# One step in 72 of an edge loop gets its table rows through SyncE, row by row

## The reference

```python
q = (X @ Wq)[src]
k = (X @ Wk)[dst]
e = jnp.tanh(q + k)                      # 64 wide
scores = e @ Wphi
exp_scores = jnp.exp(scores - jnp.max(scores))
denom = segment_sum(exp_scores, src)
alpha = exp_scores / (denom[src] + 1e-09)
msg = alpha[:, None] * ((X @ Wy_w + Wy_b)[dst] + e @ We)
out = segment_sum(msg, src)
return layernorm(x + out)
```

## Time and profile before

| what | us |
|---|---|
| median of 3 runs (5638.15, 5648.86, 12187.95) | 5648.86 |
| profiled execution | 5649.77 |
| its span in the trace | 5648.0 |

### The profile page before, as it was taken

One profiled execution on the slowest core, in us unless ns is written; L12 is line 12 of the kernel. 1 busy time (PEld: TensorE's weight loads), 2 busy tenths in 40 slices (PEclk: granted clock), 3 DMA queues, 4 the chain that ended last, 5 costly groups with the idle time before them and its releaser, 6 DMA issues. The chain is left out here.

```text
span 5648.0 us, 99340 instructions
## 1 busy us (share of the span) xinstructions
PE 4178.2 (74%) x26293; PEld 3164.3 (56%) x26293; DVE 3638.0 (64%) x8199; ACT 2776.5 (49%) x10974; POOL 3497.5 (62%) x3560
## 2 busy tenths in 40 slices
PE   7899999995676666666666666666766666676677
PEld 6745555553555555555555555555555555555556
DVE  6588888886555555555555555555555555655556
ACT  3488888884343344444444444444444434434346
POOL 1022333233777777777777777777777777777771
PEclk9956666665877777777777777778777777777778
DMA  2200000002333333333333333333333333333334
GB/s 85 70 4 4 4 4 5 4 4 59 105 105 105 105 104 105 105 105 105 105 105 105 105 105 105 105 105 105 105 106 105 105 104 105 105 105 105 105 98 108
DMA packets 279601, 478.59 MB, mean 85 GB/s; under 512 B 91964, under 2 KB 198878, under 8 KB 278814
## 3 DMA queue, kind: packets, MB, share of 16 engines
q0 software_dynamic: 166144, 326.27, 21.7%
q1 hardware_dynamic: 95132, 140.96, 7.8%
q10 hardware_dynamic: 17794, 4.91, 0.4%
HBM read 456.42 MB, written 20.60 MB: 84 GB/s over the span
## 5 line engine op out<-in xcount | busy, mean ns | idle before, releaser
L1015 POOL DMA_INDIRECT gathered<-table,dst_rows x3296 | 3156.7, 958 | 1035.0 <-issue 967.3
L1050 PE MATMUL bank<-gathered,weighted_onehots 128*128 128x193 f32 x6592 | 1793.8, 432 | 364.1 <-DVE block_sums L1122 350.4
L1039 PE MATMUL bank<-q_parts,src_onehots_T 128*128 x9888 | 1136.3, 216 | 983.9 <-DVE src_onehots_T L1084 728.8
L1050 PEld LDWEIGHTS bank<-gathered,weighted_onehots 128*128 128x128 f32 x6592 | 1497.5, 255 | 420.9 <-ACT weighted_onehots L1070 347.1
L1039 PEld LDWEIGHTS bank<-q_parts,src_onehots_T 128*128 128x128 bf16 x9888 | 870.0, 107 | 1410.0 <-issue 1208.6
L1122 DVE TENSOR_TENSOR block_sums<-block_sums,bank 128x193 f32 x3296 | 1166.1, 354 | 527.3 <-issue 193.6
L1059 ACT ACTIVATE gathered<-gathered 128x256 f32<-128x256 f32 x824 | 346.0, 420 | 2190.3 <-DVE gathered L1098 2190.3
L1070 ACT ACTIVATE weighted_onehots<-src_onehots,edge_weight 128x128 f32<-128x128 bf16 x3296 | 1073.4, 396 | 26.8
L1098 DVE TENSOR_TENSOR gathered<-bank,gathered 128x256 f32<-128x256 f32 x824 | 349.5, 424 | 1125.8 <-DMA gathered<-table,dst_rows 1107.6
L797 ACT ACTIVATE places_past_far<-bank,stat 128x98 bf16<-128x98 f32 x2727 | 887.3, 401 | 130.0 <-DVE place_col L780 93.0
L839 POOL DMA_INDIRECT sorted_list<-sorted_groups,unit_destinations x248 | 319.7, 1289 | 813.3 <-DVE sorted_groups L767 749.5
(11 more groups left out here) (180 smaller groups left out, 2248.7 us busy)
## 6 DMA issues: line engine op xcount, KB each, us to landing
src_in_block_rows<-src_in_block_list SPq DMA_DIRECT2D x206, 512.0 KB, 3.8
gathered<-table,dst_rows POOLq DMA_INDIRECT x3296
table<-in_x SPq DMA_DIRECT2D x4, 1562.5 KB
x_in<-in_x SPq DMA_DIRECT2D x24, 256.0 KB, 2.9
x_again<-in_x SPq DMA_DIRECT2D x48, 128.0 KB, 2.3
out<-out_rows SPq DMA_DIRECT2D x48, 128.0 KB, 1.9
sorted_list<-sorted_groups,unit_destinations POOLq DMA_INDIRECT x248, 2.5
table<-k_and_q ACTq DMA_DIRECT2D x24, 128.0 KB, 2.0
```

The costliest lines, as they stand in the source:

```text
L1015: e.indirect_dma_start(slot[:, r, j, 0:ROW], None, table, bass.IndirectOffsetOnAxis(ap=gidx[:, t:t + 1].bitcast(u32), axis=0)).then_inc(ga ...
L1039: made = e.matmul(QK[q % 2][:, j * A:(j + 1) * A], ohT[:, c % 2, o:o + PARTS], q3[:, bass.ds(b + s_ * A, A)], start=s_ == 0, stop=s_ == 2)
L1050: made = e.matmul(SM[q % 2 * 2 + j // 2][:, o:o + SUMS], ohw[:, q % 3, j, :], slot[:, r, j, A:SLOT], start=True, stop=True)
```

## The change

The last step of each period of 72 steps (PERIOD = 18 chunks) is no longer fetched by POOL. For these NSP = 11 steps (71, 143, ..., 791) SyncE issues 512 DMAs of one row each, 5,632 in all, into a sixth slot that only they use. Each takes its row number from a register. 16 registers are loaded at a time from `rows_for_sync`, a small tile that one more DMA reads from the sorted list and one VectorE instruction shifts right by 8. The rows of a period go out in its chunks 2 to 17, 32 rows behind each chunk's `src_in_block_rows` DMA, and the first of them (in every period but the first) waits until the step of the period before is `totalled`. The ring of `src_in_block_rows` goes from 3 to 2. POOL's five slots are counted over its own 813 steps.

```diff
-        RING, LOB = 5, 3
-        slot = sb(lists, "gathered", [PARTS, RING, QUAD, SLOT], f32)
+        RING, LOB = 5, 2
+        PERIOD = 18 * QUADS_PER_CHUNK
+        STEP_ROWS = QUAD * PARTS
+        NSP = -(-NT // CHUNK) * QUADS_PER_CHUNK // PERIOD
+        slot = sb(lists, "gathered", [PARTS, RING + 1, QUAD, SLOT], f32)
+        sync_rows = sb(lists, "rows_for_sync", [NSP, STEP_ROWS], i32)
...
+            e.dma_start(sync_rows[:, :], slist[0:NSP * PERIOD * STEP_ROWS // 1, :].rearrange("(i s) u -> i (s u)", i=NSP)
+                        [:, (PERIOD - 1) * STEP_ROWS:PERIOD * STEP_ROWS]).then_inc(sync_list_loaded, 16)
...
+            e.wait_ge(sync_list_loaded, 16)
+            e.tensor_scalar(sync_rows[:, :], sync_rows[:, :], 8, None, ALU.logical_shift_right).then_inc(sync_rows_made, 1)
...
+        def by_sync(q):
+            return q // PERIOD < NSP and q % PERIOD == PERIOD - 1
+
+        def pool_no(q):
+            return q - min(q // PERIOD, NSP)
...
+        def slot_of(q):
+            return RING if by_sync(q) else pool_no(q) % RING
+
+        def wait_for_rows(e, q):
+            if by_sync(q):
+                e.wait_ge(rows_by_sync[q // PERIOD % 4], 16 * STEP_ROWS * (q // PERIOD // 4 + 1))
+            else:
+                e.wait_ge(gathered[pool_no(q) % RING], 16 * QUAD * (pool_no(q) // RING + 1))
...
-        def sync_steps(e, first, end, limit):
+        def sync_steps(e, regs, first, end, limit):
+            if first == 0:
+                e.wait_ge(sync_rows_made, 1)
+                e.wait_ge(table_x_stored, 16 * TX)
             for q in range(first, min(end, limit), QUADS_PER_CHUNK):
                 c = q // QUADS_PER_CHUNK
                 if c >= LOB:
                     e.wait_ge(onehots_T_made, c - LOB + 1)
...
+                i = q // PERIOD
+                if i < NSP:
+                    share = 2 * CHUNK
+                    r0 = (q % PERIOD // QUADS_PER_CHUNK - 2) * share
+                    if r0 == 0 and i:
+                        e.wait_ge(totalled, i * PERIOD)
+                    for r in range(max(r0, 0), min(r0 + share, STEP_ROWS), CHUNK):
+                        e.load(regs, sync_rows[i:i + 1, r:r + CHUNK])
+                        for m in range(CHUNK):
+                            row = e.snap(regs[m], min_val=0, max_val=N)
+                            p_ = (r + m) % PARTS
+                            e.dma_start(slot[p_:p_ + 1, RING, (r + m) // PARTS, 0:ROW],
+                                        table[bass.ds(row, 1), :]).then_inc(rows_by_sync[i % 4], 16)
 
         def gpsimd_steps(e, first, end, limit):
             for q in range(first, min(end, limit)):
-                r = q % RING
-                if q >= RING:
-                    e.wait_ge(totalled, q - RING + 1)
+                if by_sync(q):
+                    continue
+                r = slot_of(q)
+                if pool_no(q) >= RING:
+                    e.wait_ge(totalled, pool_step(pool_no(q) - RING) + 1)
```

More of the change, by code:

```diff
@@ L873, in gnn_program @@
         list_turned, list_out_vector, list_out_scalar, low_kept = sem("list_turned"), sem("list_out_vector"), sem("list_out_scalar"), sem("low_kept")
-        list_rows_made = sem("list_rows_made")
+        list_rows_made, sync_list_loaded, sync_rows_made = sem("list_rows_made"), sem("list_for_sync_loaded"), sem("rows_for_sync_made")
         lows_masked, lows_made, lows_stored = sem("lows_masked"), sem("lows_made"), sem("lows_stored")
@@ L954, in gnn_program @@
         gathered = [sem(f"gathered_{i}") for i in range(RING)]
+        rows_by_sync = [sem(f"rows_by_sync_{i}") for i in range(4)]
         lows_loaded = [sem(f"src_in_block_rows_loaded_{i}") for i in range(LOB)]
@@ L964, in gnn_program @@
         leave = {k: sem(f"pass_next_{k}") for k in ENGINES if k != "sync"}
-        pass_sems = [*gathered, *lows_loaded, sums_cleared_vector, onehots_made, onehots_T_made, queried, added_qk, tanh_made,
+        pass_sems = [*gathered, *rows_by_sync, *lows_loaded, sums_cleared_vector, onehots_made, onehots_T_made, queried, added_qk, tanh_made,
                      times_phi, scored, weights_made, weighted, totalled, accumulated, row_max, core_max, shift_made, eps_made, *steps_over.values()]
@@ L971, in gnn_program, with pool_step @@
         TAIL = 5
+        def by_sync(q):
+            return q // PERIOD < NSP and q % PERIOD == PERIOD - 1
+        def pool_no(q):
+            return q - min(q // PERIOD, NSP)
+        def pool_step(n):
+            q = n
+            while pool_no(q) < n or by_sync(q):
+                q += 1
+            return q
+        def slot_of(q):
[5 more added lines that the diff above has]
+                e.wait_ge(gathered[pool_no(q) % RING], 16 * QUAD * (pool_no(q) // RING + 1))
         def block_registers(e, name):
@@ L1019, in gpsimd_landed @@
             for r in range(RING):
-                uses = len(range(r, end, RING))
+                uses = len(range(r, pool_no(end), RING))
                 if uses:
@@ L1094, in vector_steps @@
                 if 0 <= q < limit:
-                    r = q % RING
+                    r = slot_of(q)
                     e.wait_ge(queried, q + 1)
-                    e.wait_ge(gathered[r], 16 * QUAD * (q // RING + 1))
+                    wait_for_rows(e, q)
                     e.tensor_tensor(slot[:, r, :, ROW:ROW + A], QK[q % 2][:, 0:QUAD * A].rearrange("p (j f) -> p j f", f=A), slot[:, r, :, 0:A],
@@ L1101, in vector_steps @@
                 if 0 <= q < limit:
-                    r, k = q % RING, q % 2
+                    r, k = slot_of(q), q % 2
                     e.wait_ge(tanh_made, q + 1)
@@ L1321, in _ @@
             rounds, used_tiles = pass_count(e, "sync")
+            regs = block_registers(e, "sync_row")
             with e.Fori(0, rounds):
-                in_parts(e, lambda first, end, limit: sync_steps(e, first, end, limit), used_tiles, None)
+                in_parts(e, lambda first, end, limit: sync_steps(e, regs, first, end, limit), used_tiles, None)
                 over(e, "sync")
```

## The result

The changed kernel takes 5599.1 us (median of 4 runs, 5590.8 to 5601.8) against 5648.4 before: ratio 0.9913, interval [0.9899, 0.9927]. That is 49 us less (41 to 57), inside the range, 5 us above the forecast. One of the four runs of the kernel before took 12,188 us, and the ratio leaves it out. Two later groups of runs of the same program, beside the kernel before on one chip, give 45 and 51 us less. But on another chip this kernel is 12.5% slower than before, and most of what follows is about that.

What follows compares the result with a forecast made beforehand. The prediction took POOL's rate of issue, 1.262 us a gather, to set the pace. From 5649.8 us it took 55.5 for 44 gathers and added 0 to 1, all other terms costing 0: 5594 us, range 5588 to 5690.

Steps and rivals of the forecast that it cites:

- POOL's term: POOL's gathers: 44 fewer at 1.262 us each, all on the path, save 55.5 us.
- The consumers: After a period's last POOL step, VectorE and PE take two steps' rows at once, lagging at most about 4.1 us: cost 0.
- The 5.3 us of slack: Time between the totals POOL needs and its gather, in a chunk's tightest step: 5.3 us, enough for a 4.1 us lag.
- SyncE's price: SyncE's time for one row (issue 0.38, address 0.10, register load 0.07): 0.55 us, bounds 0.35 and 0.92; cost 0 below 0.667.
- The list and the smaller ring: The row-number list's DMA and VectorE instruction, and the ring of 2: cost 0, for the list at most 1 us.
- The DMA engines: Row packets, up to 16 a row, take 2% of the 16 engines, or 14% at a gather's price: cost 0.
- Rival A: SyncE is late, p above 0.667, and POOL fills its ring and stops: 5951 us at 0.73, 7020 at 0.92; chance 0.21.
- p: SyncE's price of one row DMA with its address and register load, taken as 0.55 us.
- its formula: A late SyncE needs 512p + 17 us a period; the excess over POOL's 363.4 counts 11 times.
- the overhead: SyncE's time per period besides its 512 rows: 5.8 chunk DMAs, 2 landing, 9 add to totals, together 17 us.
- Rival B: SyncE's register loads are dear, 3.0 us or more per 16: 5600 to 5700 us, 5670 for 3.2 us; chance 0.04.

Runs made afterwards that it cites:

- fetched_twice: The changed kernel with POOL also fetching the 11 steps that SyncE fetches, and the engines reading POOL's slots: 7226.9 us, ratio 1.1345 to the kernel before.
- no_rows: The changed kernel without its row DMAs, POOL fetching all 824 steps: 6361.1 us against 6365.9 for the kernel before, ratio 0.9997.

## Why the prediction was right, and where it was thin

*POOL's term* was right. 44 gathers at 1.262 us are 55.5; the profiled pair shows them, whole. Between medians 49, 45, 51 and (with four slots) 49.5 us are left, so 5 to 10 us of the term are missing. Where they go is open. The added row DMAs may disturb the gathers a little; fetched_twice was to tell, and its chip could not.

*The consumers* were right at the default ring: add distances of 3.9 and 3.0 us (4.1 and 2.9 foretold), the wait back after three steps. The 5.3 us of slack were no exact budget, as the ring of four shows: the old kernel lost 31 us with a slot less, where 0 to 11 were expected, and the changed one lost no more, where 20 to 45 more were.

*SyncE's price* was right within 0.05 us: 0.499 against 0.55. The DMA with its gap is cheaper than taken, the address dearer (0.42 for both, 0.48 foretold), the load 0.08 against 0.07. The first row in the kernel (0.43 for the issue alone) would have been the wrong one to go by.

*The list and the smaller ring* cost nothing: shown by no_rows, on a slow chip.

*The DMA engines* cost nothing either, with two packets a row where up to 16 were allowed for. The 14% of the prediction are misworked: 90,112 packets of 118 ns over 16 engines are 665 us, 12% of the span.

*Rival A* got 0.21 for a p above 0.667. The mechanism and its place were right, and its formula came within 2% of the measured times at p = 0.925 and 1.12. A part of that closeness is chance: the overhead was 12 us too small, some 7 of them of the slow chip's making, and the formula was fed the first chip's period. What failed is what p was thought to be: one number of the kernel, to be had from its rows. It also depends on where the kernel runs. On a slow chip the kernel before loses 13%, and the changed one, whose cover was 4 us in 20, loses 28% against the first chip. So that the first measurement lies in the range is luck in one respect: the forecast never asked which chip it would be made on, and on either slow chip it would have been far outside.

*Rival B* is out: a load of 16 registers takes 1.21 us, 76 ns a register. The 200 ns a register that the Trainium skill (Runtime: NRT & Kernel Launch, Instruction fetch mechanics) gives don't hold for this load from on-chip memory.

Untried: a version with more steps through SyncE, or one past the limit, on a chip where a row takes 0.50 us. By an estimate from the trace (512 x 0.50 + 17 = 273 of 298 us) 13 steps would fit there and save 10 us more; on a slow chip that version is 8% behind the changed kernel.

## What to carry to other kernels

When one queue's issue rate sets the pace, a share of its work handed to an idle queue comes off the path one to one, until that queue is late for something else that it carries. Work out that limit as a price per item, and look at how steep it is behind it: here 1% was to be won, and by the estimate each 0.01 us of price past 0.667 costs as much again. Keep the transfers that everything waits for ahead of the bulk in the queue, and measure such a kernel on more than one chip.

## What the runs showed of the hardware

- The same kernel differs by 13% between chips: the kernel before takes 5637 to 5649 us in the first measurement and on one chip of the experiments, and 6366 to 6374 on the two others. On those the granted TensorE clock is 0.67 in the mean in place of 0.75. The queues of TensorE and, where it has many instructions, SyncE halt for 0.7 us at a time, with instructions of 1 to 30 ns in bursts between the halts; POOL's median gather stays at 946 ns. What makes them halt isn't shown. Nor is it shown that the chip is the reason and not the hour: no chip was seen both ways. Every run here, on either kind of chip, was also recorded, so whether an unrecorded run halts isn't known.
- The median gather was 949 ns in two executions and 946 or 947 in the others, which over 3,276 gathers is 10 us, as much as lies between the fastest and the slowest of the first four runs of the changed kernel.
- A row of 768 bytes at an address from a register costs SyncE 0.42 us, from HBM into one partition; fetched in two pieces it cost 0.41 us more where SyncE sets the pace.
